# Six spacer buffers ahead of TensorE's operands in a three-layer Perceiver block

## The chip, the core and the metric

One core of one Trainium2 chip runs the whole program in one launch. The metric is the device time of the launch in microseconds (us). The time before is the median of three runs, 525.88 us (524.97 to 526.21).

## The reference

Three residual layers follow one another on `x` of 32 sequences of 32 tokens of width 256:

```
x = x + xattn(layernorm(x), ctx, mask)   # 16 heads of 16, ctx has 257 rows per sequence
x = x + attn(layernorm(x))               # causal, rotary, 16 heads
x = x + ffn(layernorm(x))                # top-2 of 8 experts, capacity 32 per sequence group of 128 tokens
```

An expert computes `gelu(x w0) * (x w1)` with a hidden width of 1368 and multiplies it with `wo`. All is float32.

## The kernel before

**The product in three parts.** For the large products, each operand is kept as two rounded halves, a high one and a low one (names in `_hi` and `_lo`, type fp32r), and `product3` (L224 to L228) adds three matmuls in one PSUM bank: high weights with low data, low weights with high data, high with high. The first operand of `pe.matmul` after the target is the stationary one: TensorE loads it (LDWEIGHTS, 128 columns) and then streams the second, the moving one (MATMUL, 256 columns here). The profile names a matmul as out<-moving,stationary.

**What is read together.** TensorE loads the weights of the next matmul while the moving operand of the matmul before it still streams. So in a run of `product3` calls on one pair of tensors, a stationary tensor and a moving tensor are being read from SBUF at the same time.

**The stages.** After an opening (weights turned and split), a loop over 32 context sequences runs cross attention: `turn_ctx` (four transposes), `keys` (12 matmuls, stationary `WT`, moving `ctxT`), `energies` (`Qb`, `KT`), `turn_probs` (eight transposes of `Pr`), `values` (12 matmuls, stationary `ctxT`, moving `WT`), `outputs` (`V`, `PT`). Spread between these, for each of eight tiles of 128 tokens, are `project_cross` (6 matmuls, stationary `OT`, moving `WT`), `project_self` (12 and 6, stationary `yT`, moving `WT`) and `project_out` (6, stationary `O2T`, moving `WT`). The order is written out by hand in `step`. A tail with the routing follows, and then the experts: 8 experts of 11 tiles of the hidden width, 88 tiles in all. For each tile `up` issues 12 matmuls (stationary `W01`, moving `XT`) and `down` 6 (stationary `hid_hi`/`hid_lo`, moving `W2`); ScalarE and VectorE split the next `W01` and gate the hidden tile, GpSimd splits `W2`, and SP's queue loads the next expert. At the end `combine` runs 32 matmuls (`CT`, `Y`).

**Where the buffers lie.** `sb` allocates buffers in the order of the calls. Each begins where the one before it ended, rounded up to 32 bytes per partition; a closed scope (`early`, `prep` and others) gives its bytes back, so that later buffers start again where the scope began. Every step by which the large products address their operands (a tile of 64, 128 or 256 columns of 4 bytes) apart from the 32-column ones is a multiple of 128 bytes in `WT`, `ctxT`, `OT`, `yT`, `O2T`, `XT`, `W01`, `W2` and `hid`, so the distance of two operands modulo 128 is that of their tensors' starts. The starts before, modulo 128:

| tensor | start | tensor read together with it | start | distance |
|---|---|---|---|---|
| `ctxT_hi`, `ctxT_lo` | 96 | `WT_hi`, `WT_lo` | 0 | 32 |
| `OT_hi`, `OT_lo` | 64 | `WT` | 0 | 64 |
| `yT_hi`, `yT_lo` | 0 | `WT` | 0 | 0 |
| `O2T_hi`, `O2T_lo` | 64 | `WT` | 0 | 64 |
| `W01_hi`, `W01_lo` | 32 | `XT` | 32 | 0 |
| `hid_hi`, `hid_lo` | 32 | `W2` | 32 | 0 |
| `xnT` of the first and second half of the tokens | 64, 32 | `WT` | 0 | 64, 32 |
| `Pr`, `ctx_raw`, `qk`, `pr2` (transposed) | 64, 96, 0, 0 | `tab` (identity) | 0 | 64, 32, 0, 0 |

Of the kernel before, what the change touches and what calls it, by code (L numbers as in the profile page):

```python
# [13 lines left out]
P = 128  # L14
# [45 lines left out]
def build(nc, x, ctx_in, mask, weights, xbq, xbk, xbv, xbo, router, w0, w1, wo, table, out):  # L60
    with ExitStack() as stack:
        program(nc, stack, x, ctx_in, mask, weights, xbq, xbk, xbv, xbo, router, w0, w1, wo, table, out)


def program(nc, stack, x, ctx_in, mask, weights, xbq, xbk, xbv, xbo, router, w0, w1, wo, table, out):
    def sb(name, shape, dt=F32, scope=stack):
        return scope.enter_context(nc.sbuf_tensor(name, shape, dt))

    def f(ap):

        return ap.bitcast(F32)


    tab = sb("tab", [P, NC_])
    at = [0]

# [5 lines left out]
    cos16, sin8, nsin8 = column(DH), column(DH // 2), column(DH // 2)  # L82
    causal, block, expert_no, slot_no = column(BT * S), column(HP), column(E), column(E * CAP)
    ones = sb("ones", [P, P])
    half = sb("half", [P, TT])
    zero = sb("zero", [P, E])
    WT_hi = sb("WT_hi", [P, 8, KH, D], F32R)
# [44 lines left out]
    early = ExitStack()  # L132
# [7 lines left out]
    sb("before_w_raw", [P, 10696], scope=prep)  # L140
    w_raw = sb("w_raw", [P, 8, KH, D], scope=prep)
    prep.close()
    ctxT_hi = sb("ctxT_hi", [P, 2, KH, 2 * P], F32R, early)
    ctxT_lo = sb("ctxT_lo", [P, 2, KH, 2 * P], F32R, early)
    KT = sb("KT", [P, 2, KH, SC + 1], scope=early)
    Qb = sb("Qb", [P, 2, KH, HP, S], scope=early)
    Sc = sb("Sc", [P, 2, G, SC + 1], scope=early)
    Pr = sb("Pr", [P, 2, G, SC + 1], scope=early)
    nmax = sb("nmax", [P, 2, G], scope=early)
    PT = sb("PT", [P, 2, 2, G, P], scope=early)  # L150

# [5 lines left out]
    ln_mv = {w: sb("ln_mv" + w, [P, 2], scope=early) for w in "bc"}  # L157
    ln_r = {w: sb("ln_r" + w, [P, 1], scope=early) for w in "bc"}
    y1, y2 = sb("y1", [P, D], scope=early), sb("y2", [P, D], scope=early)
    yT_hi, yT_lo = sb("yT_hi", [P, KH, P], F32R, early), sb("yT_lo", [P, KH, P], F32R, early)  # L160
    qk_s = sb("qk_s", [P, 2 * NH, DH], scope=early)
    qk = sb("qk", [P, 2 * D], scope=early)
# [2 lines left out]
    sc2 = sb("sc2", [P, G, BT, S], scope=early)  # L165
    pr2 = sb("pr2", [P, G, BT, S], scope=early)
    mx2, sum2, inv2 = (sb(n, [P, NH], scope=early) for n in ("mx2", "sum2", "inv2"))
    O2T_hi, O2T_lo = sb("O2T_hi", [P, KH, P], F32R, early), sb("O2T_lo", [P, KH, P], F32R, early)
    yTf = sb("yTf", [P, KH, P], scope=early)

# [12 lines left out]

    raw01 = sb("raw01", [P, 2, KH, HF])
    raw2 = sb("raw2", [P, HT, D])
    W01_hi, W01_lo = sb("W01_hi", [P, RW, 2, KH, P], F32R), sb("W01_lo", [P, RW, 2, KH, P], F32R)
    CT = sb("CT", [P, TT, 2, P])
    act = sb("act", [P, RH, SL])
    W2_hi, W2_lo = sb("W2_hi", [P, RW, D], F32R), sb("W2_lo", [P, RW, D], F32R)
    hid = sb("hid", [P, RH, SL])  # L190
    hid_hi, hid_lo = sb("hid_hi", [P, RW, SL], F32R), sb("hid_lo", [P, RW, SL], F32R)
    Y = sb("Y", [P, TT, 2, D])

# [2156 lines left out]
```

How the kernel before makes its waits and increments, by code:

```python
    def free_slot(eng, n):  # L242
        if n >= len(ROOM):
            eng.wait_ge(sm["first_act"], n - len(ROOM) + 1)
            eng.wait_ge(sm["first_dve"], sum(by_dve[:n - len(ROOM) + 1]))
# [5 lines left out]
    def split_ready(eng, e, t):  # L252
        for c, (t0, t1) in enumerate(CH):
            if t == t0:
                eng.wait_ge(raw_in[c], 16 * RAW_DMAS[c] * (e + 1))
# [96 lines left out]
    def wait_freed(eng, name, half_, n, ring):  # L353
        eng.wait_ge(sm[name], max(NT * half_ + n - ring + 1, 0) + 1)
# [52 lines left out]
        def load_ctx(j):  # L409
            for u in range(4):
                b = 4 * j + u
                if beyond(b, 6):
                    move_stats(b - 6, (u - 6) % 4)
                sp.wait_ge(sm["ctx_turned"], b - 3)
                src = ctx_in[bass.ds(b, 1), 0:2 * P, :] if not isinstance(b, int) else ctx_in[b:b + 1, 0:2 * P, :]
                sp.dma_start(ctx_raw[:, u, :, :], src.rearrange("a (t p) d -> p (a t) d", p=P)).then_inc(ctx_in_sem[u], 16)
# [1 line left out]
        def move_stats(b, r):  # L418
            if isinstance(b, int) and b >= LATE:
                sp.wait_ge(sm["p_ready"], 4 * b + 4)
            else:
                sp.wait_ge(sm["p_normed"], b + 1)
            t = b // BT if isinstance(b, int) else (b - r) // BT
            rows = last_prob[r * S:(r + 1) * S, one(t)].rearrange("p a h k -> p (a h) k").rearrange("p (g h) k -> p g h k", h=HG)
            for h in range(HG):
                sp.dma_start(rows[:, :, h, :], Pr[h * S:(h + 1) * S, r % 2, :, SC - 1:SC + 1]).then_inc(stats_moved[r % 2], 16)
```

## Time and profile before

| | |
|---|---|
| median of 3 runs | 525.88 us |
| the profiled execution's own time | 525.44 us |
| its span, first to last instruction | 523.7 us |
| outside the span | 1.7 us |
| granted TensorE clock, mean | 0.987 |
| TensorE busy (matmuls) | 489.7 us, 94% |
| VectorE busy | 390.7 us, 75% |
| ScalarE busy | 323.8 us, 62% |
| GpSimd busy | 271.8 us, 52% |

Matmul records overlap: each is some 0.28 us long from its start to the end that the profile gives it, while the next starts about 0.12 us after it. So the length of a run of matmuls is read from the starts: last start less first start, over the number of steps between them. This is called the step below.

### The profile page before, as it was taken

Reading aid. Unit: us, or ns where it says so; the run is one execution under the profiler, and the core shown is the slowest. Engines: PE = TensorE matmul, PEld = TensorE weight load, DVE = VectorE, ACT = ScalarE, POOL = GpSimd, SP = SyncE. Lnnn points to the kernel's source line nnn. Section 1 sums busy time; section 2 is a strip of 40 time slices with the busy share of each in tenths; the row PEclk is TensorE's granted clock in tenths of the full one; section 3 lists DMA queues with packets and bytes.
Section 4 is the critical chain, followed back from the end, with each engine's and each line's share of the span. In section 5 each row is a group of like instructions: output and inputs, shape, how many; then the busy total and the mean of one; then the engine's idle time right before and its main releaser. Section 6 shows DMA issues by size and latency. Waiting matters only on the chain.

```text
span 523.7 us, 18399 instructions
## 1 busy us (share of the span) xinstructions
PE 489.7 (94%) x6699; PEld 450.7 (86%) x6699; DVE 390.7 (75%) x987; ACT 323.8 (62%) x838; POOL 271.8 (52%) x362
## 2 busy tenths in 40 slices
PE   1898999899999999999998779999999999999997
PEld 1777888788888888888886669999999999999996
DVE  2545546576766767767678988989989998999984
ACT  1447766675766757766674256666666666666651
POOL 4134444436345364343644272998656666666660
PEclk9979999999999999999999997999999999999999
DMA  6623111111211101111003600466555646465402
GB/s 174 196 72 95 24 43 44 25 43 44 44 22 41 40 21 41 20 41 21 3 4 87 240 2 0 129 197 222 165 181 182 176 166 203 124 199 189 134 1 81
DMA packets 58126, 48.92 MB, mean 93 GB/s; under 512 B 20942, under 2 KB 49744, under 8 KB 58064
## 3 DMA queue, kind: packets, MB, share of 16 engines
q1 hardware_dynamic: 58064, 48.09, 31.7%
q8 instruction: 40, 0.66, 0.5%
q14 instruction: 22, 0.18, 0.1%
HBM read 46.86 MB, written 1.08 MB: 92 GB/s over the span
## 4 chain that ended last, share of the span: by engine, by line
PE 79%; issue 6%; DVE 5%; ACT 4%; DMA 3%; SPq 1%; POOL 1%; ACTq 0%; DVEq 0%; POOLq 0%
PE bank L226 20%; PE bank L228 18%; PE bank L227 18%; PE bank L647 5%; PE bank L615 3%; PE bank L668 3%; PE bank L572 2%; ACT Pr L1150 2%; DMA w_raw<-in_L_xattn_Wk 2%; DMA last_prob<-Pr 1%; PE bank L1046 1%; PE bank L925 1%; PE bank L804 1%; ACT PTd L1243 1%; PE bank L764 1%
## 5 line engine op out<-in xcount | busy, mean ns | idle before, releaser
L226 PE MATMUL bank<-XT_lo,W_hi 128*128 128x256 f32 (+1 forms) x352 | 99.3, 282 | 0.3 <-DVE XT_lo L1916 0.3
L227 PE MATMUL bank<-XT_hi,W_lo 128*128 128x256 f32 (+1 forms) x352 | 99.0, 281 | 0.0
L228 PE MATMUL bank<-XT_hi,W_hi 128*128 128x256 f32 (+1 forms) x352 | 98.8, 281 | 0.0
L2319 POOL TENSOR_TENSOR W_lo<-raw,W_hi 128x256 fp32r<-128x256 f32 (+1 forms) x88 | 84.4, 959 | 7.0
L2201 POOL TENSOR_TENSOR Pr<-Pr,rinv 128x1028 f32<-128x1028 f32 (+2 forms) x32 | 60.5, 1889 | 48.5 <-DVE rinv L1496 47.7
L1150 ACT ACTIVATE Pr<-Sc,nmax 128x257 f32<-128x257 f32 x128 | 63.8, 502 | 22.0 <-DVE nmax L1485 19.5
L1485 DVE CUSTOM_DVE_ANT_0 Sc<-bank,mask_add 128x257 f32<-128x257 f32 x128 | 47.0, 423 | 40.5 <-PE bank L615 17.6
L1956 DVE TENSOR_TENSOR W_lo<-raw,W_hi 128x512 fp32r<-128x512 f32 (+1 forms) x88 | 71.7, 815 | 5.0 <-ACT W_hi L1317 1.4
L2317 POOL CAST W_hi<-raw 128x256 fp32r<-128x256 f32 (+1 forms) x88 | 43.5, 495 | 53.3 <-PE bank L228 32.7
L2128 DVE TENSOR_TENSOR hid_lo<-hid,hid_hi 128x256 fp32r<-128x256 f32 (+1 forms) x88 | 68.7, 781 | 1.5 <-ACT hid_hi L1392 1.5
L226 PEld LDWEIGHTS bank<-XT_lo,W_hi 128*128 128x128 f32 (+1 forms) x352 | 65.4, 186 | 0.4 <-issue 0.4
L227 PEld LDWEIGHTS bank<-XT_hi,W_lo 128*128 128x128 f32 (+1 forms) x352 | 65.2, 185 | 0.0
L228 PEld LDWEIGHTS bank<-XT_hi,W_hi 128*128 128x128 f32 (+1 forms) x352 | 65.2, 185 | 0.0
L1388 ACT ACTIVATE act<-bank 128x256 f32<-128x256 f32 (+1 forms) x88 | 33.6, 382 | 45.8 <-PE bank L228 45.4
L1317 ACT ACTIVATE W_hi<-raw 128x512 fp32r<-128x512 f32 (+1 forms) x88 | 53.9, 612 | 0.0
L226 PE MATMUL bank<-W_lo,hid_hi 128*128 128x256 f32 (+1 forms) x176 | 50.1, 285 | 0.2 <-issue 0.2
L227 PE MATMUL bank<-W_hi,hid_lo 128*128 128x256 f32 (+1 forms) x176 | 49.5, 281 | 0.0
L228 PE MATMUL bank<-W_hi,hid_hi 128*128 128x256 f32 (+1 forms) x176 | 49.5, 281 | 0.0
L1392 ACT ACTIVATE hid_hi<-hid 128x256 fp32r<-128x256 f32 (+1 forms) x88 | 36.8, 419 | 16.2 <-DVE hid L2123 15.1
L2123 DVE TENSOR_TENSOR hid<-bank,act 128x256 f32<-128x256 f32 (+1 forms) x88 | 36.5, 415 | 9.9 <-ACT act L1388 9.5
L226 PE MATMUL bank<-WT_lo,ctxT_hi 128*128 128x256 f32 x128 | 39.6, 309 | 1.0 <-ACT KT L1127 0.8
L1140 ACT ACTIVATE V<-bank 128x512 f32<-128x512 f32 x32 | 19.1, 597 | 32.9 <-PE bank L228 32.9
(248 smaller groups left out, 1349.0 us busy)
## 6 DMA issues: line engine op xcount, KB each, us to landing
raw<-in_L_ffn_w_kernel SPq DMA_DIRECT2D x32, 512.0 KB, 4.6
ctx_raw<-in_ctx SPq DMA_DIRECT2D x32, 256.0 KB, 2.8
raw<-in_L_ffn_wo_kernel SPq DMA_DIRECT2D x16, 512.0 KB, 5.7
raw<-in_L_ffn_w_kernel SPq DMA_DIRECT2D x16, 344.0 KB
last_prob<-Pr SPq DMA_DIRECT2D x128, 1.0 KB, 1.8
raw<-in_L_ffn_wo_kernel SPq DMA_DIRECT2D x8, 256.0 KB
x_sb<-in_x SPq DMA_DIRECT2D x4, 256.0 KB, 5.8
VL_all<-vl_rows SPq DMA_DIRECT2D x8, 128.0 KB
```

Of the source, the lines that this page charges most:

```text
L226: pe.matmul(dst, a_hi, b_lo, start=first, stop=False)
L227: pe.matmul(dst, a_lo, b_hi, start=False, stop=False)
L228: return pe.matmul(dst, a_hi, b_hi, start=False, stop=last)
L1150: ac.activation(Pr[:, r % 2, g, 0:SC], Sc[:, r % 2, g, 0:SC], ACT.Exp, bias=nmax[:, r % 2, g:g + 1], scale=-1.0, accum_out=Pr[:, r % 2, g, ...
L1317: ac.activation(W01_hi[:, (NT * half_ + n) % RW, :, :, 0:w].rearrange("p i k n -> p (i k) n"), raw01[:, :, :, t * P:t * P + w].rearrange(" ...
L1392: ac.activation(hid_hi[0:w, m % RW, :], hid[0:w, m % RH, :], ACT.Copy).then_inc(sm["hhi_done"], 1)
L1485: ve.tensor_tensor_reduce(Sc[:, r % 2, g, 0:SC], bk[g][:, 0:SC], mask_add[:, :], -0.25, 3e38, ALU.add, ALU.min, nmax[:, r % 2, g:g + 1]).t ...
L1956: ve.tensor_tensor(W01_lo[:, (NT * half_ + n) % RW, :, :, 0:w].rearrange("p i k n -> p (i k) n"), raw01[:, :, :, t * P:t * P + w].rearrang ...
L2128: ve.tensor_tensor(hid_lo[0:w, m % RW, :], hid[0:w, m % RH, :], f(hid_hi[0:w, m % RW, :]), ALU.subtract)\
L2201: po.tensor_tensor(Pr[:, r % 2, own, 0:n], Pr[:, r % 2, own, 0:n], rinv[:, r % 2, own].unsqueeze(2).broadcast_to([P, own.stop - own.start, ...
L2317: po.tensor_copy(W2_hi[0:w, m % RW, :], raw2[0:w, t, :]).then_inc(sm["hi2"], 1)
L2319: po.tensor_tensor(W2_lo[0:w, m % RW, :], raw2[0:w, t, :], f(W2_hi[0:w, m % RW, :]), ALU.subtract)\
```

## The change

Six buffers that nothing reads or writes are allocated: 96 bytes per partition ahead of `ctxT`, 32 ahead of `nmax`, 64 ahead of `yT`, 64 ahead of `O2T`, 64 ahead of `W01` and 64 ahead of `hid_hi`. No instruction is added, removed or moved. What follows a spacer in its scope is moved up by its bytes. The starts after, modulo 128: `ctxT` 64, `OT` 64, `yT` 64, `O2T` 64, `W01` 96, `W2` 96, `hid_hi` and `hid_lo` 32, with `WT` at 0 and `XT` at 32 as before. So all six pairs named in the first six lines of the table are 64 apart. `xnT` and `ctx_raw` stay; `Pr` goes from 64 to 32, `qk` and `pr2` from 0 to 64, `CT` from 32 to 96 with `Y` at 32. Two pairs stay 0 apart: the last matmul of `up` streams `XT` (32) while `hid` (32) is loaded, and the last of `down` streams `W2` (96) while `W01` (96) is loaded.

```diff
@@ program @@
     prep.close()
+    sb("apart_ctxT", [P, 24], scope=early)
     ctxT_hi = sb("ctxT_hi", [P, 2, KH, 2 * P], F32R, early)
...
     Pr = sb("Pr", [P, 2, G, SC + 1], scope=early)
+    sb("apart_OT", [P, 8], scope=early)
     nmax = sb("nmax", [P, 2, G], scope=early)
...
     y1, y2 = sb("y1", [P, D], scope=early), sb("y2", [P, D], scope=early)
+    sb("apart_yT", [P, 16], scope=early)
     yT_hi, yT_lo = sb("yT_hi", [P, KH, P], F32R, early), sb("yT_lo", [P, KH, P], F32R, early)
...
     mx2, sum2, inv2 = (sb(n, [P, NH], scope=early) for n in ("mx2", "sum2", "inv2"))
+    sb("apart_O2T", [P, 16], scope=early)
     O2T_hi, O2T_lo = sb("O2T_hi", [P, KH, P], F32R, early), sb("O2T_lo", [P, KH, P], F32R, early)
...
     raw2 = sb("raw2", [P, HT, D])
+    sb("apart_W01", [P, 16])
     W01_hi, W01_lo = sb("W01_hi", [P, RW, 2, KH, P], F32R), sb("W01_lo", [P, RW, 2, KH, P], F32R)
...
     hid = sb("hid", [P, RH, SL])
+    sb("apart_hid", [P, 16])
     hid_hi, hid_lo = sb("hid_hi", [P, RW, SL], F32R), sb("hid_lo", [P, RW, SL], F32R)
```

## Rows read from the trace of the kernel before

**Rows 1.** The page's chain that ended last, by engine.

```profile
PE 79%; issue 6%; DVE 5%; ACT 4%; DMA 3%; SPq 1%; POOL 1%; ACTq 0%; DVEq 0%; POOLq 0%
```

**Rows 2.** Stretches: length, busy us and records of PE, PEld, DVE, ACT, POOL; clock; DMA.

```profile
120.00:150.00 30.00, 28.65 (x563) 25.33 (x563) 19.94 (x65) 21.07 (x62) 14.57 (x19) 1.00 0.15 30
280.00:300.00 20.00, 15.05 (x309) 13.02 (x308) 18.03 (x63) 5.58 (x14) 5.09 (x8) 1.00 0.66 212
440.00:480.00 40.00, 40.00 (x339) 40.00 (x338) 38.22 (x60) 26.36 (x61) 27.58 (x38) 1.00 0.56 172
```

**Rows 3.** The page's groups: count, busy us, mean ns, idle before them and its releaser.

```profile
L226 PE MATMUL bank<-XT_lo,W_hi 128*128 128x256 f32 (+1 forms) x352 | 99.3, 282 | 0.3 <-DVE XT_lo L1916 0.3
...
L2123 DVE TENSOR_TENSOR hid<-bank,act 128x256 f32<-128x256 f32 (+1 forms) x88 | 36.5, 415 | 9.9 <-ACT act L1388 9.5
```

**Rows 4.** TensorE in order of time, one expert tile, `up` then `down`: start, length us.

```profile
400.64 0.28 PE L226 MATMUL bank<-XT_lo,W_hi 128*128 128x256 f32 x1
...
401.00 0.28 PE L226 MATMUL bank<-XT_lo,W_hi 128*128 128x256 f32 x1
401.12 0.28 PE L227 MATMUL bank<-XT_hi,W_lo 128*128 128x256 f32 x1
...
402.78 0.28 PE L226 MATMUL bank<-XT_lo,W_hi 128*128 128x256 f32 x1
```

**Rows 5.** The weight loads in order of time, same tile.

```profile
401.01 0.19 PEld L227 LDWEIGHTS bank<-XT_hi,W_lo 128*128 128x128 f32 x1
```

**Rows 6.** TensorE in order of time, `keys`, then `values`, second to twelfth matmul.

```profile
122.98 0.28 PE L227 MATMUL bank<-ctxT_hi,WT_lo 128*128 128x256 f32 x1
...
124.18 0.28 PE L228 MATMUL bank<-ctxT_hi,WT_hi 128*128 128x256 f32 x1
...
126.88 0.28 PE L227 MATMUL bank<-WT_hi,ctxT_lo 128*128 128x256 f32 x1
...
128.06 0.28 PE L228 MATMUL bank<-WT_hi,ctxT_hi 128*128 128x256 f32 x1
```

**Rows 7.** TensorE in order of time, `project_self` of 12, first and last.

```profile
147.56 0.28 PE L226 MATMUL bank<-WT_lo,yT_hi 128*128 128x256 f32 x1
...
148.87 0.28 PE L228 MATMUL bank<-WT_hi,yT_hi 128*128 128x256 f32 x1
```

**Rows 8.** TensorE in order of time, `project_out` of two tiles, first and last of six.

```profile
154.61 0.28 PE L226 MATMUL bank<-WT_lo,O2T_hi 128*128 128x256 f32 x1
...
155.17 0.28 PE L228 MATMUL bank<-WT_hi,O2T_hi 128*128 128x256 f32 x1
...
218.52 0.28 PE L226 MATMUL bank<-WT_lo,O2T_hi 128*128 128x256 f32 x1
...
219.11 0.28 PE L228 MATMUL bank<-WT_hi,O2T_hi 128*128 128x256 f32 x1
```

**Rows 9.** TensorE in order of time, `project_cross`, first, fourth and last of six.

```profile
139.95 0.28 PE L226 MATMUL bank<-WT_lo,OT_hi 128*128 128x256 f32 x1
...
140.31 0.28 PE L226 MATMUL bank<-WT_lo,OT_hi 128*128 128x256 f32 x1
...
140.54 0.28 PE L228 MATMUL bank<-WT_hi,OT_hi 128*128 128x256 f32 x1
```

**Rows 10.** TensorE in order of time, `queries` of the first, then the second token half.

```profile
20.05 0.40 PE L227 MATMUL bank<-xnT_hi,WT_lo 128*128 128x512 f32 x1
...
22.35 0.39 PE L228 MATMUL bank<-xnT_hi,WT_hi 128*128 128x512 f32 x1
...
60.52 0.39 PE L227 MATMUL bank<-xnT_hi,WT_lo 128*128 128x512 f32 x1
...
61.45 0.40 PE L228 MATMUL bank<-xnT_hi,WT_hi 128*128 128x512 f32 x1
```

**Rows 11.** TensorE in order of time, transposes, merged: start, length of all, count.

```profile
78.28 1.03 PE L647 MATMUL bank<-tab,Pr 128*128 128x128 f32 x8
...
112.34 0.60 PE L572 MATMUL bank<-tab,ctx_raw 128*128 128x128 f32 x4
```

## The prediction

> **What bounds the kernel now.** I read the chain that ended last first: 79% of it is TensorE [rows 1]. The stretches say where. In the experts' stage TensorE is busy in 40.00 of 40 us at the full granted clock, and in the cross-attention loop in 28.65 of 30 us; only the tail between them is VectorE's (18.03 of 20 us, TensorE 15.05) [rows 2]. The groups by line confirm it for the experts: all 352 first matmuls of `product3` on `XT` waited 0.3 us together, while VectorE stood idle 9.9 us ahead of its gating, mostly for ScalarE's gelu [rows 3]. So in the experts' stage (some 190 us) and most of the loop (some 250 us), a shorter step between matmuls is a shorter kernel, nearly one to one. Neither queues nor waits are touched by the change; it can act only through how long an access takes.
>
> **What the change could act on.** A weight load starts at 401.01, 10 ns after the matmul ahead of its own (401.00), and its own starts at 401.12 [rows 4, 5]. So stationary and moving operand are read at the same time during the whole step, as the change supposes. The trace of before holds pairs at all three distances in one and the same form (128x128 weights, 256 columns), which is an experiment of its own. I take the step in each:
>
> Distance 0, experts: 18 steps from 400.64 to 402.78, 2.14/18 = 118.9 ns [rows 4]. Distance 0, `yT`: 11 steps from 147.56 to 148.87, 1.31/11 = 119.1 ns [rows 7]. Distance 32, `keys`: 1.20/10 = 120.0 ns; `values`: 1.18/10 = 118.0 ns; I take 119.0 for both [rows 6]. Distance 64, `O2T`: 0.56/5 = 112 ns in one tile and 0.59/5 = 118 in another [rows 8]; of the five tiles in the undisturbed loop three go like the first and two like the second. Distance 64, `OT`: 0.59/5 = 118 ns in six tiles, but the first three steps take 0.36 (120 each) and the last two 0.23 (115 each) [rows 9]. The mean over these eleven groups is (3 x 0.56 + 2 x 0.59 + 6 x 0.59)/11 = 0.582 us for five steps, 116.4 ns.
>
> `O2T` and `yT` are both small stationary tensors against moving `WT`, in the same loop and partly back to back; the distance is the plainest difference between them. That is why I take the 64-apart mean, 116.4 ns, for the steps that the change sets 64 apart. It is not the best value seen (112 to 113), because two groups of five never reached that, and it is not zero gain, because nothing at distance 0 or 32 shows a whole group at 112.
>
> **The sum.** Experts: of a tile's 18 steps, 16 come to 64 apart (two stay at 0, at the passage between `up` and `down`). 88 x 16 = 1408 steps x (118.9 - 116.4) = 3.5 us. `keys` and `values`: 64 groups of 12, 11 steps inside each, 704 x (119.0 - 116.4) = 1.8 us. `yT`: eight tiles with 11 and 5 inner steps, 128 x (119.1 - 116.4) = 0.35 us. `OT` and `O2T` are 64 apart before and after: nothing. Together 5.7 us. In the loop TensorE is busy 95% of the time [rows 2], so of the 2.2 us there I count 2.1: 5.6 us in all. From the profiled execution's own 525.44 this gives 519.8 us. The median of the runs lies 0.44 above that execution, so on the scale of the medians I predict 520.3 us.
>
> The edits whose cost I set at nothing: the spacers have no instruction. The transposes of `Pr` go from 64 to 32 apart; eight of them at 64 take 1.03 us, less the 0.28 of the last, over 7 = 107 ns a step, and four of `ctx_raw` at 32 take (0.60 - 0.28)/3 = 107 ns [rows 11], so the distance shows no price there (if it had one of 2.5 ns, 256 steps would cost 0.6 us, which the low side of the gain has room for). `Qb` and `KT`, `V` and `PT`, `kT` and `qTb` keep their distance. The other engines' operands move by 32 to 256 bytes too, `W01` against `raw01` and `hid` against `hid_hi` on VectorE among them. No row shows what that does; VectorE has 1.78 us of 40 spare in the experts [rows 2], so up to 4% longer operations there are hidden, and beyond that it becomes the bound. In the loop it is busy 19.94 of 30 us, and TensorE covers it.
>
> **A rule that speaks against it.** The rows give a step of 118.9 ns at distance 0 and 112 in some groups at 64 [rows 4, 8]. The Trainium skill, page SBUF — State Buffer, section "Who interferes with whom", says that TensorE has two independent read ports, one for the moving operand and one for the weights, and that "PE and ACT never wait on anyone". By it the change is worth 0 and the time stays at 525.9; by the rows it is worth 5.6 us. The trace so far speaks against the rule, but with eleven short groups.
>
> **The rivals.** *A, the forecast*: the pooled step, 520.3 us; by the scatter of the eleven groups, 516 to 524.8.
>
> *B, the steps lock at the best value.* In three `O2T` groups all five steps, and in `OT` the last two, are at 112 to 115. Runs of 12 give more room to settle than runs of 6. At 113 ns: 1408 x 5.9 + 704 x 6.0 + 128 x 6.1 = 8.3 + 4.2 + 0.8 = 13.3 us, 512.6 us on the medians' scale. Against it: the two `O2T` groups that stayed at 118, and the two passages in each expert tile that stay at 0 and start the settling anew. VectorE would then be a bound too: 16 x 5.9 = 94 ns off a tile of 2.14 us is 4.4%, and VectorE's spare is 1.78/40 = 4.4%.
>
> *C, the distance does nothing.* Then the differences above come from the place of the groups in the loop. For it: the 512-column steps of `queries` are 2.30/10 = 230 ns at distance 64 and 0.93/4 = 232 at 32 [rows 10], less than 1% between them, and the second kind of `O2T` group at 118 is what `values` has at 32. 525.9 us, within 1 us.
>
> *D, slower: the steps never settle.* The first three steps after a passage into `OT` take 120 ns, more than the 118.9 of the experts at distance 0, where the stream stays at one distance throughout. The change brings two changes of distance into each tile, where there was none. If the unsettled 120 ns held for all steps of the change, 1408 x 1.1 + 704 x 1.0 + 128 x 0.9 = 2.4 us would be added: 528.2 us. It decides as soon as the mean step at 64 is above 118.9. Against it: `OT` settles after three steps.
>
> **How the numbers follow.** A 0.50, B 0.18, C 0.20, D 0.12. A measurement of this kernel tells 0.2%, about 1 us, from no change. Faster is A and B, 0.68; C gives 0.19 to the same and 0.01 to slower; D is slower, so slower is 0.13. The range leaves out D and the outer edges of B and C: 512.5 to 526.5 us. A's own range is 516 to 524.8.
>
> **What would show it.** In the profile of the changed kernel, the 18 steps of an expert tile should take some 2.10 us in place of 2.14 (2.14 says C, 2.04 says B, 2.16 says D), and a stretch of 40 us should hold 345 matmul records in place of 339. Steps of `yT` should fall from 119 towards 116, those of `O2T` and `OT` stay. VectorE's share in the experts should rise as the stage gets shorter. The prediction is wrong if the steps inside `up` do not fall, or if they fall and VectorE's waits take the gain back.

## The result and the profile after

The changed kernel takes 523.22 us (median of 22 runs, 518.48 to 526.07) against 525.7 for the kernel before (22 runs, 524.13 to 529.73). The ratio is 0.9937, with a 95% interval of 0.9912 to 0.9962: some 3.3 us (2.0 to 4.6) faster. The means, 522.97 and 526.27 us, stand in that ratio; the medians are 2.5 us apart. The profiled execution took 519.11 us with a span of 517.3 us, so it is one of the fastest of its kernel; what can be read from it is where time went, not how much was won on the median. Of the 6.3 us between the two profiled executions 3.4 are the experts' and 1.5 the loop's; of the rest, a part goes with the clock, which was granted at half ahead of the experts for 6.8 us in the execution before (315.7 to 322.5 us) and for 3.4 in this one.

The expert tile is where the change shows best. TensorE in order of time in the changed kernel, one tile from the first matmul of `up` on, and the `down` ahead of it (L233 to L235 are `product3`, seven lines further down than before):

```profile
399.92 0.28 PE L233 MATMUL bank<-W_lo,hid_hi 128*128 128x256 f32 x1
...
400.63 0.28 PE L233 MATMUL bank<-XT_lo,W_hi 128*128 128x256 f32 x1
...
402.04 0.28 PE L233 MATMUL bank<-W_lo,hid_hi 128*128 128x256 f32 x1
```

The 18 steps from 399.92 to 402.04 take 2.12 us, where they took 2.14 [rows 4]; this tile is one of the slower kind. Over longer stretches (columns as in [rows 2]) the count of matmul records says it better, 346 in 40 us where there were 339:

```profile
400.00:440.00 40.00, 40.00 (x346) 40.00 (x345) 37.51 (x62) 26.49 (x61) 26.36 (x39) 1.00 0.61 194
440.00:480.00 40.00, 40.00 (x346) 40.00 (x346) 38.55 (x63) 26.59 (x61) 26.84 (x39) 1.00 0.57 181
```

VectorE's share rose from 38.22 to 38.55 of 40 us as its work came in a shorter time, and TensorE still did not wait: the row that answers to [rows 3] has the same 0.3 us ahead of its 352 matmuls.

```profile
L233 PE MATMUL bank<-XT_lo,W_hi 128*128 128x256 f32 (+1 forms) x352 | 98.3, 279 | 0.3 <-DVE XT_lo L1923 0.3
```

In the loop, `project_self` of 12 (order of time, first and last, one tile later than in [rows 7]) went from 119 to 1.25/11 = 113.6 ns a step (the mean over all `yT` steps from 119.2 to 114.6); `keys` (second to twelfth) from 120 to 1.15/10 = 115; `values` stayed at 1.18/10 = 118 [rows 6]:

```profile
178.37 0.28 PE L233 MATMUL bank<-WT_lo,yT_hi 128*128 128x256 f32 x1
...
179.62 0.28 PE L235 MATMUL bank<-WT_hi,yT_hi 128*128 128x256 f32 x1
```

```profile
122.30 0.28 PE L234 MATMUL bank<-ctxT_hi,WT_lo 128*128 128x256 f32 x1
...
123.45 0.28 PE L235 MATMUL bank<-ctxT_hi,WT_hi 128*128 128x256 f32 x1
...
126.06 0.28 PE L234 MATMUL bank<-WT_hi,ctxT_lo 128*128 128x256 f32 x1
...
127.24 0.28 PE L235 MATMUL bank<-WT_hi,ctxT_hi 128*128 128x256 f32 x1
```

From here on "stage" is the experts' time from the first matmul on `XT` to the last on `hid`, and "step" the mean distance of successive starts in it (those under 130 ns, to leave out the real pauses). Before: stage 190.7 us, step 118.7 ns. After: 187.3 us, 116.5 ns. The first and last starts of the changed kernel's two tensors, as its trace groups them by tile (min/median/max duration in ns, first to last start):

```profile
L233 PE MATMUL bank<-XT_lo,W_hi x352: 276/280/357, 320.7 to 504.8; 128*128 128x256 f32 x160, 128*88 128x256 f32 x16
...
L235 PE MATMUL bank<-W_hi,hid_hi x176: 277/281/283, 325.4 to 508.0; 128*128 128x256 f32 x160, 88*128 88x256 f32 x16
```

### The profile page after: what moved, and what is told of

Same layout as the page of the kernel before. It is cut to its first block, busy times and chain, and to the rows that moved or that the text cites. A ratio compares the mean times of both kernels' runs of the same rounds, so it can differ in the third digit from the quotient of the medians.

```text
span 517.3 us, 18399 instructions
## 1 busy us (share of the span) xinstructions
PE 482.8 (93%) x6699; PEld 443.2 (86%) x6699; DVE 390.6 (76%) x987; ACT 323.2 (62%) x838; POOL 270.5 (52%) x362
## 4 chain that ended last, share of the span: by engine, by line
PE 78%; issue 6%; DVE 5%; ACT 5%; DMA 3%; SPq 1%; POOL 1%; DVEq 0%; ACTq 0%; POOLq 0%
PE bank L233 20%; PE bank L235 18%; PE bank L234 18%; PE bank L654 5%; PE bank L622 3%; PE bank L675 3%; PE bank L579 2%; ACT Pr L1157 2%; DMA w_raw<-in_L_xattn_Wk 1%; PE bank L1053 1%; DMA last_prob<-Pr 1%; ACT PTd L1250 1%; PE bank L811 1%; PE bank L771 1%; SPq L434 1%
## 5 line engine op out<-in xcount | busy, mean ns | idle before, releaser
L233 PE MATMUL bank<-XT_lo,W_hi 128*128 128x256 f32 (+1 forms) x352 | 98.3, 279 | 0.3 <-DVE XT_lo L1923 0.3
L235 PE MATMUL bank<-XT_hi,W_hi 128*128 128x256 f32 (+1 forms) x352 | 97.9, 278 | 0.0
L234 PE MATMUL bank<-XT_hi,W_lo 128*128 128x256 f32 (+1 forms) x352 | 97.8, 278 | 0.0
L2135 DVE TENSOR_TENSOR hid_lo<-hid,hid_hi 128x256 fp32r<-128x256 f32 (+1 forms) x88 | 70.5, 801 | 1.7 <-ACT hid_hi L1399 1.5
L2324 POOL CAST W_hi<-raw 128x256 fp32r<-128x256 f32 (+1 forms) x88 | 41.9, 476 | 50.9 <-PE bank L235 31.9
L233 PEld LDWEIGHTS bank<-XT_lo,W_hi 128*128 128x128 f32 (+1 forms) x352 | 65.2, 185 | 0.5 <-issue 0.5
L235 PEld LDWEIGHTS bank<-XT_hi,W_hi 128*128 128x128 f32 (+1 forms) x352 | 65.0, 185 | 0.0
L233 PE MATMUL bank<-W_lo,hid_hi 128*128 128x256 f32 (+1 forms) x176 | 50.0, 284 | 0.2 <-issue 0.2
L235 PE MATMUL bank<-W_hi,hid_hi 128*128 128x256 f32 (+1 forms) x176 | 49.3, 280 | 0.0
L233 PE MATMUL bank<-WT_lo,ctxT_hi 128*128 128x256 f32 x128 | 39.5, 308 | 1.1 <-ACT KT L1134 0.9
```

The costliest lines, as they stand in the source:

```text
L233: pe.matmul(dst, a_hi, b_lo, start=first, stop=False)
L234: pe.matmul(dst, a_lo, b_hi, start=False, stop=False)
L235: return pe.matmul(dst, a_hi, b_hi, start=False, stop=last)
L2135: ve.tensor_tensor(hid_lo[0:w, m % RW, :], hid[0:w, m % RH, :], f(hid_hi[0:w, m % RW, :]), ALU.subtract)\
L2324: po.tensor_copy(W2_hi[0:w, m % RW, :], raw2[0:w, t, :]).then_inc(sm["hi2"], 1)
```

## The experiments

Two theories stood against each other. The distance theory: the step is set by how far apart, modulo 128, the two operands lie that TensorE reads together. The rival: it is something else that moving the buffers brought. The diffs are against the changed kernel. Each kernel was timed in alternation with the kernel before, those with 48 and 80 bytes in one run each.

**All buffers moved, all distances kept.**

```diff
-    sb("apart_ctxT", [P, 24], scope=early)
+    sb("apart_ctxT", [P, 32], scope=early)
...
-    sb("apart_hid", [P, 16])
+    sb("apart_hid", [P, 32])
```

(all six spacers alike). 

> All six spacers are made 128 bytes, so every buffer behind them is moved but all distances modulo 128 are those of the kernel before. Theory (the distance sets the step): the expert tile stays at 2.14 us for 18 steps (118.7 ns), 339 matmul records in 40 us, ratio to before 0.998 to 1.002. Rival (what counts is that the buffers were moved, or what moved beside them on the other engines): the step falls to about 116.5 ns as in the changed kernel, ratio 0.994.

Measured: ratio 1.0006 (0.9981 to 1.003), stage 191.7 us, step 119.3 ns. Moving alone gives nothing: the rival falls. The step is even 0.7 ns longer than before (119.34 against 118.67), where an unchanged one was expected. The stretch in the experts, columns as in [rows 2]:

```profile
440.00:480.00 40.00, 40.00 (x337) 40.00 (x336) 38.14 (x61) 26.24 (x60) 27.61 (x38) 1.00 0.53 167
```

**The experts' spacers alone, and the loop's alone.**

```diff
-    sb("apart_ctxT", [P, 24], scope=early)
-    sb("apart_OT", [P, 8], scope=early)
-    sb("apart_yT", [P, 16], scope=early)
-    sb("apart_O2T", [P, 16], scope=early)
```

> Only the spacers ahead of W01 and hid are kept. Theory: the experts' stage is 3.4 us shorter (190.7 to 187.3 us from its first to its last matmul), the loop stays at 243.8 us; ratio 0.993 to 0.995. Rival (the gain comes from the loop and from where the half-clock stretch falls in the tail): experts' stage under 1 us shorter, ratio above 0.997.

Measured: ratio 0.9926 (0.9901 to 0.9951), stage 187.9 us, step 116.4 ns. The whole gain of the change is here, as far as the intervals can tell. Its loop took 245.6 us in place of the expected 243.8; the reason follows with the next kernel.

```diff
-    sb("apart_W01", [P, 16])
...
-    sb("apart_hid", [P, 16])
```

> Only the four spacers in the loop's scope are kept. Theory: the loop from first to last energies is 1.5 us shorter (243.8 to 242.3 us), the experts' step stays at 118.7 ns; ratio 0.995 to 0.998. Rival (all of the gain is the experts'): loop unchanged, ratio 1.000.

Measured: ratio 0.9999 (0.9967 to 1.003), step in the experts 118.7 ns. The steps in the loop did fall (mean in `keys` 115.1 ns, `yT` 114.2, `values` 117.4), and the time did not. On the ratio the rival came out (1.000) and the theory (0.995 to 0.998) did not; on the loop both missed: 245.6 us in the profiled execution, where 242.3 or an unchanged 243.8 was expected. TensorE's line in order of time at the loop's beginning, with the idle time before it, and the stretch behind it show what was in the way:

```profile
46.87 1.11 PE L577 MATMUL bank<-tab,ctx_raw 128*128 128x128 f32 x4 [2.71 <-DMA ctx_raw<-in_ctx]
```

```profile
47.00:54.00 7.00, 7.00 (x95) 6.61 (x96) 1.18 (x2) 4.04 (x13) 1.00 (x3) 0.55 0.18 44
```

One context sequence came 2.71 us late (0.88 in the kernel before, 0.81 in the changed one), and behind this lull the clock was granted at 0.55 of 2.4 GHz for 7 us. That is not the spacers' doing: the kernel with the experts' spacers alone waited 2.97 us at the same place, and one further down without the loop's spacers 3.23 us, with a loop of 246.6 us. Against that one, which also had 6.8 us at the lower level, the loop with spacers is 1.0 us shorter, of which 0.5 is the shorter wait for the sequence; the first of the two, with 3.4 us at the lower level, has a loop just as long, 245.6 us.

**All 18 steps of a tile 64 apart.** One more spacer takes `W2` and with it `hid_hi` to places where the two passages fit as well.

```diff
+    sb("apart_W2", [P, 16])
     W2_hi, W2_lo = sb("W2_hi", [P, RW, D], F32R), sb("W2_lo", [P, RW, D], F32R)
```

> One spacer of 64 bytes more, ahead of W2: W01 starts at 96, W2 at 32, hid_hi and hid_lo at 96 modulo 128, XT at 32, so that the two passages between up and down in each expert tile are 64 apart as well, all 18 steps. Theory (a passage at distance 0 throws the stream out of the 113 ns step and it needs up to a whole run to come back): the mean step in the experts falls from 116.4 to 113 to 114 ns, the stage from 187.3 to 180 to 184 us, 350 to 354 records in 40 us; ratio to before 0.982 to 0.989. Rival 1 (the two passages are just two steps of 18): step 116 ns, stage 186.7 us, ratio as the changed kernel's. Rival 2 (VectorE becomes the bound): TensorE waits for hid or W01 appear, VectorE 39.5 of 40 us busy, stage not under 185 us.

Measured: 520.48 us, ratio 0.9882 (0.984 to 0.9923): the lowest median of this study, though with six runs its interval overlaps the changed kernel's. What tells the two apart is the profile: stage 184.4 us, step 114.5 ns, 352 records in 40 us. Step and stage are just above the 113 to 114 ns and 180 to 184 us of the theory. TensorE's steps, `down` and the beginning of `up`, then the stretch:

```profile
400.65 0.28 PE L234 MATMUL bank<-W_lo,hid_hi 128*128 128x256 f32 x1
...
401.33 0.28 PE L234 MATMUL bank<-XT_lo,W_hi 128*128 128x256 f32 x1
...
402.58 0.28 PE L236 MATMUL bank<-XT_hi,W_hi 128*128 128x256 f32 x1
```

```profile
440.00:480.00 40.00, 40.00 (x352) 40.00 (x351) 39.33 (x64) 27.22 (x63) 27.19 (x39) 1.00 0.58 180
```

From 400.65 to 402.58 are 17 steps in 1.93 us, 113.5 ns, through the passage at 401.33 without a break. Two steps changed their distance, yet all 18 gained: the stage lost 2.9 us, and two steps of 18 at 5 ns less are 0.9 us. So a passage at 0 unsettles the run behind it. The rows of steps show it: in the changed kernel runs of `up` go by turns at 118 and at 114 ns, while here 1165 of 1568 steps are 113 or 114 ns. What still breaks the run here is the last, narrow tile of each expert (88 rows of weights and of data in `down`); after it three runs take 118. VectorE has 0.67 of 40 us left, and TensorE waited 0.2 us for `hid_lo` in the stretch from 320 to 510 us.

**The same without the loop's spacers.** The changed kernel's four loop spacers left out, `apart_W2` put in.

> The loop's four spacers are left out; in the experts all 18 steps of a tile are 64 apart (W01 at 96, W2 at 32, hid_hi and hid_lo at 96, XT at 32). Theory (the time comes from the experts; the loop's spacers add next to nothing): the experts' stage is about 184.4 us as with all spacers and 18 steps, step 114.5 ns; ratio to before 0.986 to 0.990, no worse than with the loop's spacers. Rival (the loop's shorter steps count for 1.5 to 2 us): ratio 0.991 to 0.993.

Measured: 520.82 us, ratio 0.9891 (0.9853 to 0.9928), stage 184.4 us, step 114.5 ns. The loop's spacers make no difference that the intervals can tell.

**Other distances.** As the last kernel, with spacers of `[P, 8]`, `[P, 24]`, `[P, 8]` ahead of `W01`, `W2` and `hid_hi` for 32 bytes, and `[P, 24]`, `[P, 8]`, `[P, 24]` for 96.

> As the kernel with 18 steps and no loop spacers, but weights 32 bytes from the moving operand instead of 64 (W01 at 64, W2 at 32, hid at 64, XT at 32). Theory (the step goes by the distance and 64 is best): step 117.5 to 119.5 ns as in keys and values of the kernel before, stage 189 to 191.5 us, ratio 0.998 to 1.002. Rival (any distance but 0 will do): step 114 to 115 ns, stage 184.5 us, ratio 0.988.

> The same with 96 bytes (W01 at 0, W2 at 32, hid at 0, XT at 32). Theory (a distance counted modulo 128, the same as 32 the other way round): step within 1 ns of that of distance 32, 117.5 to 119.5 ns, ratio 0.998 to 1.002. Rival (the weights' lag counts in one direction): a step that differs from that of distance 32 by 2 ns or more.

Measured: at 32 ratio 0.9999 (0.9972 to 1.0025), stage 191.3 us, step 119.1 ns; at 96 ratio 0.995 (0.9925 to 0.9975), stage 188.4 us, step 117.2 ns. The expectation that 32 and 96 would be one and the same failed: they differ by 1.9 ns, and by 3.1 on `XT` alone (119.7 and 116.6). On `hid` alone they are alike (118.4 and 118.5), so that the direction counts is shown for the runs on `XT` only.

For 48 and 80, with the loop's spacers, `W01` and `hid` were made 128 bytes longer and used from their 16th byte on (`hid` like `W01` below), with spacers of `[P, 8]`, `[P, 24]`, `[P, 8]` ahead of `W01`, `W2` and `hid_hi` for 48, and of `[P, 16]` for 80; one run each.

```diff
+    AT = 4
+    W01_hi, W01_lo = (sb(n, [P, RW * 2 * KH * P + 32], F32R)[:, AT:AT + RW * 2 * KH * P].rearrange(
+        "p (r i k n) -> p r i k n", r=RW, i=2, k=KH) for n in ("W01_hi", "W01_lo"))
```

> The loop's four spacers as in the change; in the experts the weights lie 48 bytes from the moving operand in all 18 steps (W01 and hid at 80, W2 and XT at 32). Theory (the 113 ns step needs the operands in opposite halves of 128 bytes, so 64 is the middle of what works): step between those of 32 (119.1) and 64 (114.5), 115 to 118.5 ns. Rival (only 64 settles): step 118 ns or more. For the loop: if its gain is real but partly beside other work, the steady period of four sequences is 31.7 to 31.85 us against 31.9 to 32.0 without the spacers; if the profile with 31.95 was the rule, 31.9 or more.

> The same with 80 bytes (W01 and hid at 112, W2 and XT at 32). Theory: step between those of 96 (117.3) and 64 (114.5), 114.5 to 117 ns. Rival (only 64 settles): 117 ns or more. The loop's steady period as for 48 bytes.

Measured: at 48 stage 191.1 us, step 118.9 ns (526.99 us in the one run); at 80 stage 189.9 us, step 118.1 ns (527.29 us). Both are at the rival's figure, 118 ns or more at 48 and 117 or more at 80, and the theory that 64 is the middle of a broad range got no support. What 64 bytes alone have is whole runs at 113 to 114 ns. Of the 85 runs of `up` with 12 matmuls, such a mean is found in 63 in the kernel with 18 steps, in 40 in the changed kernel, in one at 96 bytes and in none at 0, 32, 48 and 80. Single steps of 113 ns are no sign of it: 771 in the kernel with 18 steps, but also 186 at 96, 120 with all buffers moved by multiples of 128, 29 at 48 and 10 at 80. The kernels with 48 and 80 bytes also let `W01` and `hid` begin 16 bytes past a multiple of 32; what that does by itself was not tested.

**Only the passages 64 apart.** `W01` at 32 and `W2`, `hid` at 96, so that the 16 inner steps stay 0 apart.

```diff
-    sb("apart_W01", [P, 16])
...
+    sb("apart_W2", [P, 16])
...
-    sb("apart_hid", [P, 16])
```

(and without the loop's spacers). 

> The inverse of the change in the experts: the 16 inner steps of a tile stay 0 apart (W01 and XT at 32; W2 and hid at 96), only the two passages between up and down are 64 apart. Theory (each distance has its own settled step, and a passage unsettles it): step 118.5 to 119.5 ns, stage 190.5 to 192 us, ratio 1.000 to 1.005. Rival (what gained in the kernel with 18 steps was the passages as such): step under 118 ns, stage under 189.5 us, ratio under 0.997.

Measured: ratio 1.0021 (0.999 to 1.0052), stage 190.8 us, step 118.8 ns. The passages alone are worth nothing; they pay only where the steps on both sides are 64 apart.

The experts' step by distance, one profiled execution each:

| inner steps | passages | step, ns | stage, us | records in 440 to 480 us |
|---|---|---|---|---|
| 0 (before) | 0 | 118.7 | 190.7 | 339 |
| 0, all moved by multiples of 128 | 0 | 119.3 | 191.7 | 337 |
| 0 | 64 | 118.8 | 190.8 | 339 |
| 32 | 32 | 119.1 | 191.3 | 338 |
| 48 | 48 | 118.9 | 191.1 | 339 |
| 64 (after) | 0 | 116.5 | 187.3 | 346 |
| 64 | 64 | 114.5 | 184.4 | 352 |
| 80 | 80 | 118.1 | 189.9 | 341 |
| 96 | 96 | 117.2 | 188.4 | 343 |

Kernels with the same places in the experts agree closely in the step: 118.67 and 118.68 ns (before, and the loop's spacers alone), 116.45 and 116.44 (after, and the experts' alone), 114.47 and 114.51 (the two with 18 steps). So the 119.3 ns with all buffers moved by multiples of 128 is a real 0.7 more than before: the places count for a little that their distance modulo 128 does not tell. That it is the pair, and not the place of one tensor, shows on `hid`: with `hid` at 96 the steps between its matmuls take 114.3 ns with `W2` at 32 and 118.9 with `W2` at 96, and 118.6 with both at 32. What the other engines' accesses to the moved buffers add was not tested apart; that the same two values, about 113 and 118 ns, are met in the loop beside other work [rows 8] speaks against them.

## Why the prediction was right, and where its sum was too large

**That distance sets the step: right, and its size in part by luck.** The forecast was 520.3 us, 5.6 less than before; 523.22 us and a gain of 3.3 by the ratio were measured. The pooled step of the eleven `O2T` and `OT` groups, 116.4 ns, was taken for the experts' 16 steps; measured 116.5 over all 18, with 346 records in 40 us where 345 were expected. The experts' term of 3.5 us measured 3.4 (190.7 to 187.3), and the kernel with the experts' spacers alone gives the whole ratio. That the two agree to 0.1 ns is luck. In the five later kernels whose loop lies as before (the experts' spacers alone, 18 steps without the loop's spacers, 32, 96 and the passages alone), the same eleven groups give 116.6 to 117.6 ns, and with these the term would have been 1.8 to 3.2 us. And the mean is made in another way: in the loop some short groups ran at 113 and others at 118, in the experts whole runs of `up` go by turns, because of the passages at 0. `O2T` and `OT` were to stay: `OT` did (117.4 and 117.6 ns), while all five groups of `O2T` are at 113.4 in the changed kernel (115.5 in the mean before). The 112 ns of the prediction comes from starts rounded to 10 ns; unrounded it is 113.

**The loop's term: mis-sized.** It was 2.1 us on the median; alone it measures 0.0 (ratio 0.9999, 0.9967 to 1.003, so 1.7 us faster to 1.6 slower). Three parts of it show. First, `values` did not follow: 118.3 before, 117.5 after, at the same 64 bytes as `keys` (119.5 to 115.4). Second, not each nanosecond of TensorE's is on the chain. Four sequences make a period of the loop; the chain of the kernel before has the first `energies` of a period at 153.24 and three periods later at 249.09, 31.95 us each, and the changed kernel's chain is

```profile
152.28 0.62 PE bank L622 x16
...
247.68 0.62 PE bank L622 x16
```

31.80 us each: 0.15 us a period, 1.2 us in eight if all went alike. A wait shows where the rest went. Ahead of the transposes of `Pr` TensorE sits idle until, by the profile, ScalarE has written `PTd`: 0.41 us in the tile of [rows 7] and 0.53 us in the same tile of the changed kernel (the first row is the kernel before):

```profile
149.56 0.30 PE L647 MATMUL bank<-tab,Pr 128*128 128x128 f32 x1 [0.41 <-ACT PTd L1243]
148.60 0.63 PE L654 MATMUL bank<-tab,Pr 128*128 128x128 f32 x4 [0.53 <-ACT PTd L1250]
```

From the last `yT` start to this transpose it takes 0.69 to 0.73 us in the last four of these places in every kernel whose loop distances are as before, and 0.81 to 0.84 in the five whose loop operands are 64 apart: some 0.13 us of a period's shorter steps end in the wait. "TensorE is busy 95% of the time" counted records that overlap, and so took work beside the chain for work on it. Third, even this gain is not always there. In the kernel with 18 steps and in the two with 48 and 80 bytes, all with the loop's spacers, a lull of TensorE near 132 us, of 1.40 to 1.47 us, is followed by 3.4 us at the lower clock (1.2 GHz), and the period stays at 31.95 us from there on. Why it stays so after the clock is back, no run here shows. The kernel with 18 steps, order of time with the idle time before, and stretches:

```profile
132.14 0.22 PE L676 MATMUL bank<-PT,V 128*32 128x32 f32 x2 [1.47 <-issue]
```

```profile
128.00:132.00 4.00, 2.67 (x147) 2.25 (x147) 2.23 (x10) 2.23 (x7) 2.98 (x4) 1.00 0.21 66
132.00:136.00 4.00, 3.86 (x21) 3.82 (x21) 1.72 (x3) 1.69 (x7) 0.00 (x0) 0.57 0.31 66
```

The same lull is 0.85 us in the changed kernel's profile, and 0.59 to 1.38 in the nine profiles in which the clock stayed up there. But the length of the lull alone does not decide: some 32 us earlier TensorE was idle for 1.63 us in the changed kernel (below, with the stretch behind it) and for 1.75 us in the kernel with 48 bytes, and the clock stayed at 1.00.

```profile
99.24 0.32 PE L675 MATMUL bank<-PT,V 128*32 128x32 f32 x12 [1.63 <-issue]
```

```profile
100.00:104.00 4.00, 4.00 (x47) 3.71 (x47) 1.73 (x4) 2.57 (x7) 1.08 (x1) 1.00 0.09 5
```

Over the timed runs the mean granted clock was below 0.985 in 22 of 40 runs of the kernels with the loop's operands 64 apart (the two kernels of one run left out) and in 41 of 118 of the others. For the changed kernel itself, 11 runs of 22 were at 0.987 or higher, median 521.07 us, and 11 at 0.984 or lower, median 524.66; the kernel before had, beside the experiments, 37 runs of 58 at the higher value, median 525.62, and 21 at the lower, 527.87. So at the higher clock the gain was 4.6 us, near the 5.6 of the forecast, and more runs at the lower clock took a part of it back on the median. For the loop's spacers alone it was 0.5 us at the higher clock (six runs, median 525.1). A run's mean clock does not tell where in it the lower clock lay. Whether the loop's spacers cause these runs is suggested by the counts and not shown: no run here changed the lull alone, and the kernels with 32 bytes and with the passages alone, which have no loop spacers, had lulls of 1.38 and 1.36 us without a drop, and the late context sequence is followed by the lower clock in kernels of both kinds.

**What was set at nothing.** VectorE's cover held: 38.55 of 40 us. `Pr`'s transposes take 109.1 ns from start to start at 64 before and at 32 after alike (the prediction's 107 was read from merged lengths). All that moved with the buffers cost nothing that shows in the time: with all distances kept, the ratio is 1.0006.

**The rivals.** B, the locked step, was a right picture of what the operands can do (113 to 114 ns) and a wrong one of this change, since the two passages that stay at 0 undo it; with these at 64 as well it happens for three steps in four. C, that distance does nothing, is refuted by the kernel with all distances kept against the two with 64. Its argument from the 512-column steps [rows 10] did not carry over to 256 columns. D, steps that never settle, was to show in a mean step above 118.9 at 64: it is 116.5.

**The rule of the skill.** Steps of the same form, on the same engine, fell from 118.7 to 114.5 ns by the operands' places alone. The Trainium skill, page SBUF — State Buffer, section "Who interferes with whom", has TensorE's two read ports independent and TensorE waiting on nobody. The measurement decides against it for this form of operands: what counts is where the two operands lie to one another, so the two reads are not independent of each other here. What they share, no run here shows.

## What to carry to other kernels

Where TensorE is the bound and each matmul's weights are loaded under the matmul before it, look at the step between starts, not at the records' durations, and compare groups of one form whose operands lie at different distances: the trace of before held the two values, about 113 and 118 ns, that the experts' steps would take. How often each is taken it did not hold: short groups gave a mean that the next kernels did not repeat. Follow the chain of pairs through every change of operands, since one passage at the wrong distance unsettles the run behind it. And count a gain on TensorE only for the part of a stage that its chain runs through; a loop with other work on its chain, or a clock that drops after a lull, can take the rest.

## What the runs showed of the hardware

The step of a 256-column fp32r matmul has preferred values. At 64 bytes whole runs are at 113 to 114 ns: in the kernel with 18 steps 1165 of 1568 steps, most of the others at 116 to 118. At 0, 32, 48 and 80 bytes no run of 12 matmuls in `up` has such a mean, and the step lies at 118.1 to 119.3 ns. After the narrow tile of an expert three runs (30 matmuls) take about 118 before 113 to 114 returns. 32 and 96 bytes are not alike (119.1 and 117.2 ns), the difference being on `XT` alone. The distance modulo 128 is not all: moving all buffers by multiples of 128 made the step 0.7 ns longer. The transposes, at 109 ns from start to start for 32 and 64 alike, show nothing of this.
